# Key tokens first in each group, query tokens last, in a fused vision-tower kernel

## The reference

```python
h = tok(x, channel_weights)                 # patch sums, then 12 -> 192
n = layernorm(h); q, k = n[:, :64], n[:, 64:]
a = softmax(q @ k.T * scale) @ k            # per image
a = transpose(a, (0, 2, 1)).reshape(B, 64, 192) @ proj_w.T + proj_b
h = h + concat([a, k], axis=1)              # keys: only h + layernorm(h)
n = layernorm(h)
s = sigmoid(n @ gate_w.T)                   # best 2 of 4 pairs of experts, then best 2 experts
cw = s of the two chosen, over their sum
out = h + sum_e cw_e * ((silu(n @ w1_e.T) * (n @ w3_e.T)) @ w2_e.T) + the same with the shared expert
```

## Time and profile before

| what | value |
|---|---|
| median of 3 runs | 1877.27 us (1877.26 to 1882.26) |
| the profiled execution | 1882.22 us |
| its span, first to last instruction | 1880.5 us |
| granted clock of TensorE, mean | 0.925 |
| DMA | 436.58 MB, mean 232 GB/s |
| PE / DVE / ACT / POOL busy | 84% / 58% / 49% / 38% |

### The profile page before, as it was taken

The page is one execution under the profiler, slowest core; times in us unless marked ns, Lnnn a source line. Parts: engine busy times, 40 slices in busy tenths (PEclk is TensorE's granted clock), DMA queues, the critical chain, the costliest instruction groups (busy, mean ns, idle before and its releaser), DMA issues.

```text
span 1880.5 us, 30301 instructions
## 1 busy us (share of the span) xinstructions
PE 1584.0 (84%) x9350; PEld 1242.6 (66%) x9350; DVE 1091.8 (58%) x1863; ACT 916.5 (49%) x3047; POOL 705.6 (38%) x687
## 2 busy tenths in 40 slices
...
GB/s 296 314 328 245 299 241 238 278 220 300 254 251 240 255 283 266 255 252 267 234 251 242 255 282 266 254 246 269 286 244 243 257 268 61 47 95 114 86 112 93
DMA packets 120850, 436.58 MB, mean 232 GB/s; under 512 B 20109, under 2 KB 49538, under 8 KB 99182
## 3 DMA queue, kind: packets, MB, share of 16 engines
...
...
HBM read 413.86 MB, written 20.07 MB: 231 GB/s over the span
## 4 chain that ended last, share of the span: by engine, by line
PE 31%; issue 30%; POOL 13%; DVE 11%; DMA 8%; ACT 3%; SPq 3%; ACTq 0%; POOLq 0%; DVEq 0%
PE bank L1427 12%; POOL ffn L655 10%; PE bank L1276 7%; DMA xt<-in_x 7%; PE bank L1447 3%; DVE pooled L842 3%; POOL stat L630 3%; DVE ffn L1190 2%; PE bank L1373 2%; DMA ffn<-cw_rows 2%; SPq L482 1%; PE bank L1385 1%; ACT xt L700 1%; PE bank L1345 1%; PE bank L1405 1%
## 5 line engine op out<-in xcount | busy, mean ns | idle before, releaser
L655 POOL TENSOR_TENSOR ffn<-ffn 128x512 f32<-128x512 f32 (+1 forms) x448 | 515.0, 1152 | 945.9 <-ACT ffn L804 923.2
L1427 PE MATMUL bank<-W2T,ffn 128*128 128x192 f32 (+1 forms) x3600 | 701.5, 334 | 0.0
L1190 DVE TENSOR_TENSOR ffn<-bank,ffn 128x512 f32<-128x512 f32 (+1 forms) x504 | 313.3, 622 | 607.4 <-POOL ffn L655 423.7
L1427 PEld LDWEIGHTS bank<-W2T,ffn 128*128 128x128 f32 (+1 forms) x3600 | 608.7, 192 | 46.3 <-issue 4.8
L842 DVE TENSOR_REDUCE pooled<-xt 128x5 f32<-128x1280 f32 (+2 forms) x296 | 434.4, 1471 | 48.3 <-DMA xt<-in_x 47.2
L804 ACT ACTIVATE ffn<-bank 128x512 f32<-128x512 f32 (+1 forms) x504 | 273.8, 546 | 341.8 <-PE bank L1447 216.4
L700 ACT ACTIVATE xt<-xt 128x256 f32<-128x256 f32 x800 | 323.3, 410 | 184.5 <-DMA xt<-in_x 184.3
L1447 PE MATMUL bank<-tokT,Wx 126*128 126x512 bf16 (+1 forms) x720 | 240.6, 355 | 53.1 <-DVE ffn L1190 52.1
L1447 PEld LDWEIGHTS bank<-tokT,Wx 126*128 126x128 bf16 x720 | 72.1, 101 | 131.7 <-DVE ffn L1190 86.7
L700 ACT ACTIVATION_READ_ACCUMULATOR xt<-xt 128x1 f32 x800 | 155.2, 194 | 0.0
L1276 PE MATMUL bank<-x0h,WT0h 128*128 128x512 f32 x288 | 141.8, 492 | 6.9 <-issue 5.7
...
## 6 DMA issues: line engine op xcount, KB each, us to landing
xt<-in_x SPq DMA_DIRECT2D x168, 1792.0 KB, 7.6
...
out<-stage SPq DMA_DIRECT2D x192, 96.0 KB
...
```

The costliest lines, as they stand in the source:

```text
L655: nc.gpsimd.tensor_tensor(out=cwb[slot][:, 0:n], in0=silu[(g.par + step) % 2][:, 0:n], in1=cwb[slot][:, 0:n], op=ALU.mult).then_inc(scaled, 1)
L1190: v.tensor_tensor(out=h[step % HR][:, 0:n], in0=h_ps(g, step, 1)[:, 0:n], in1=(silu[p] if e == NE else cwb[(c * NE + e) % CW_RING])[:, 0:n ...
L1427: last = mm(o, h[step % HR][:, 128 * t:128 * t + m], W2T[:, e, :], start=(e == 0 and query and t % 2 == 0), stop=(e == NE), skip_group_che ...
```

## The change

- The chunks' order: five key chunks (3, 3, 4, 3 and 3.5 tiles of 128 tokens), then two query chunks. Keys are laid out in runs of 8 tokens per image, so that any number of tiles makes a chunk.
- The plan falls into two. `AK_PLAN` (steps 39 to 60) holds what the key tokens of the **next** group need: tok, V, stats, pow, X, their gates, CK, and half of U. `AQ_PLAN` (steps 0 to 36) holds what the queries of the group **itself** need, attention above all, beside its own key steps. Before group 0's first expert step only `AK_PLAN` runs.
- Tiles: 11 of group g+2 at steps 40 to 61 (`LATE`), 10 of group g+1 at steps 1 to 34 (`EARLY`), the latter in three parts. `SLOTS` is 3.
- Splitting (`Xw`, `Uw`) moves from DVE to POOL; DVE only makes the two replicas.
- Softmax: DVE subtracts each image's maximum (`S`), ACT takes one exponential for eight images (`exp`, twice per group), DVE sums (`sum`).
- `H`: a 72-row stack `Mst` is assembled by DMAs (`stack_mix`, at steps 11 and 17), and one fp32 product replaces three.
- Gates: 28 operations in place of 36, but once for keys (17 tiles) and once for queries (8 tiles). The choice of pairs compares all with all. The coefficient rows are written out by ACT's queue, not SP's.
- The last two second-layer products and the evacuation of a group move into the first steps of the next. `layer2` adds the keys' residual (L1425) in the last step of a chunk, not the first.
- X2T and UTk have one buffer each, not two. The preparation of `CWr` becomes two DMAs.

```diff
-SLOTS = 2
-
-CHUNKS = [(True, 0, 512), (True, 512, 512), (False, 0, 512), (False, 2048, 64)]
-CHUNKS += [(False, 512 * i, 512) for i in (1, 2, 3)]
+
+KT = [3, 3, 4, 3, 3.5]
+CHUNKS = [(False, int(128 * sum(KT[:i])), int(128 * n)) for i, n in enumerate(KT)] + [(True, 0, 512), (True, 512, 512)]
 TT = [(n + 127) // 128 for _, _, n in CHUNKS]
-QCH = 2
-EVAC = [sum((t + 1) // 2 for t in TT[QCH:c + 1]) for c in range(len(TT))]
+QCH = len(KT)
 KPAD = 2176
 NCH = len(CHUNKS)
 STEPS = NCH * EX
+QSTEP = QCH * EX
 GT = 8 + 17
 CWCOL = 1024 + GB * NK
-
-SHARE = {"dve": [(0, 5), (5, 9)], "act": [(9, 12), (12, NP)], "pool": None}
+SLOTS = 3
+
+SHARE_K = {"dve": [(0, 3), (3, 6), (6, 9)], "act": [(9, 11), (11, 13), (13, NP)], "pool": None}
+SHARE_Q = {"dve": [(0, 5), (5, 9)], "act": [(9, 12), (12, NP)], "pool": None}
...
+AQ_PLAN = {
+    0: [("PHT", 0), ("VHw", 0)],
+    1: [("PHT", 1), ("VHT", 0)],
+    2: [("U", 4), ("S", 0)],
+    3: [("U", 5), ("S", 1), ("VHw", 1)],
+    4: [("U", 6), ("S", 2), ("VHT", 1)],
+    5: [("U", 7), ("exp", 0)],
+    6: [("ET", 0), ("sum", 0)],
+    7: [("ET", 1)],
+    8: [("S", 3), ("AH", 0)],
+    9: [("S", 4), ("M", 0)],
+    10: [("S", 5), ("M", 1)],
+    11: [("exp", 1)],
+    12: [("ET", 2), ("sum", 1)],
+    13: [("ET", 3)],
+    14: [("AH", 1)],
+    15: [("M", 2), ("H", 0)],
+    16: [("M", 3), ("H", 1)],
+    17: [("H", 2)],
+    18: [("H", 3)],
+    19: [("stat_q", 0)],
+    20: [("x2", 0), ("H", 4)],
+    21: [("XT", 0), ("H", 5)],
+    22: [("XT", 1), ("H", 6)],
+    23: [("H", 7)],
+    24: [("stat_q", 1)],
+    25: [("x2", 1)],
+    26: [("XT", 2)],
+    27: [("XT", 3)],
+    28: [("GQ", 0), ("GQ", 1)],
+    29: [("G", 0)],
+    36: [("CQ", 0), ("CQ", 1)],
 }
-A_FIRST = 2
-GATES = 36
-for _s in range(12):
-    PLAN[45 + _s] = [("gate", n) for n in range(3 * _s, min(GATES, 3 * _s + 3))] + PLAN.get(45 + _s, [])
-ITEMS = [it for s in sorted(PLAN) for it in PLAN[s]]
-PE_KINDS = ("tok", "V", "PHT", "VHT", "S", "U", "ET", "AH", "M", "X", "H", "XT", "GQ", "G", "C")
-DVE_KINDS = ("tok", "H", "AH", "XT")
+MIX = {11: 0, 17: 1}
+A_FIRST = 39
+AK_PLAN = {
+    39: [("fin", 0), ("tok", 0), ("V", 0)],
+    40: [("stats", 0), ("pow", 0)],
+    41: [("pow", 1)],
+    42: [("stats2", 0), ("pow", 2)],
+    43: [("pow", 3)],
+    45: [("Xw", 0)],
+    46: [("Xw", 1)],
+    47: [("Xw", 2)],
+    48: [("Xw", 3)],
+    49: [("X", 0), ("X", 1)],
+    50: [("X", 2), ("X", 3)],
+    51: [("X", 4), ("X", 5), ("Uw", 0)],
+    52: [("keyG", 0), ("keyG", 1), ("GK", 0), ("Uw", 1)],
+    53: [("Uw", 2)],
+    54: [("Uw", 3)],
+    55: [("U", 0)],
+    56: [("U", 1)],
+    57: [("U", 2)],
+    58: [("U", 3)],
+    59: [("CK", 0), ("CK", 1), ("CK", 2)],
+    60: [("CK", 3), ("CK", 4)],
+}
+GATES = 28
+for _n in range(GATES):
+    AQ_PLAN.setdefault(30 + _n // 5, []).append(("gate_q", _n))
+    AK_PLAN.setdefault(53 + _n // 5, []).append(("gate_k", _n))
+ITEMS = [it for plan in (AK_PLAN, AQ_PLAN) for s in sorted(plan) for it in plan[s]]
+PE_KINDS = ("tok", "V", "PHT", "VHT", "S", "U", "ET", "AH", "M", "X", "H", "XT", "GQ", "G", "GK", "CQ", "CK")
+DVE_KINDS = ("tok", "S", "H", "AH", "XT")
 ROUNDS = [it for it in ITEMS if it[0] in PE_KINDS]
 NR = len(ROUNDS)
 R = {it: i for i, it in enumerate(ROUNDS)}
 BYDVE = [sum(1 for it in ROUNDS[:i + 1] if it[0] in DVE_KINDS) for i in range(NR)]
 BYACT = [i + 1 - BYDVE[i] for i in range(NR)]
 S_IMGS = [(0, 3), (3, 3), (6, 2), (8, 3), (11, 3), (14, 2)]
-LINKS = 57
-
-
-
-
-LATE = {s: i for i, s in enumerate([4, 6, 8, 10, 12, 13, 16, 19, 22, 25, 29, 36, 38, 41, 46, 49, 52, 55, 58])}
-EARLY = {0: 19, 1: 20}
-POOL_TILES = TILES + len(LATE)
+LINKS = 73
+WORKS = 10
+
+
+LATE = {s: i for i, s in enumerate([40, 44, 46, 48, 50, 52, 53, 55, 57, 59, 61])}
+EARLY = {s: len(LATE) + i for i, s in enumerate([1, 5, 8, 12, 16, 20, 23, 27, 31, 34])}
+assert len(LATE) + len(EARLY) == TILES and max(EARLY) + 2 < A_FIRST
...
+def items_at(g, step, left):
+
+    found = [(g, kind, i) for kind, i in AQ_PLAN.get(step, [])] if g.off >= 0 else []
+    if left:
+        found += [(g.plus(1), kind, i) for kind, i in AK_PLAN.get(step, [])]
+    return found
...
+def tile_parts(g, step, left, engine):
+
+    found = []
+    for back in (2, 1, 0):
+        for gt_, t in tiles_at(g, step - back, left):
+            parts = share(gt_, t)[engine]
+            if back < len(parts):
+                found.append((gt_, t, back, parts[back], back == len(parts) - 1))
...
-        CWr = sb("CWr", [128, 3, 4, 128])
+        CWr = sb("CWr", [3 * 2 * CH, 2 * NQ])
...
+            def stack_mix(g, half):
+
+                sp.wait_ge(aux_act, g.at(BYACT[-1], BYACT[R[("M", 2 * half + 1)]]))
+                for m in range(4):
+                    sp.dma_start(Mst[:, 4 * half + m, :],
+                                 Msb[2 * CH * m:2 * CH * (m + 1), half, :]).then_inc(mixed[half], 16)
...
+            def step_dma(g, step, left):
+
+                if step >= 61 and left:
+                    for ahead in ((0, 1) if step == 61 else (2, 3, 4)):
+                        cw_load(g.plus(1), ahead)
+                elif step + CW_AHEAD < STEPS and g.off >= 0:
+                    cw_load(g, step + CW_AHEAD)
+                if step >= LOAD_BEHIND:
+                    landed = tiles_at(g, step - LOAD_BEHIND, left) if g.off >= 0 or step - LOAD_BEHIND >= A_FIRST else []
+                else:
+                    landed = tiles_at(g.minus(1), step - LOAD_BEHIND + STEPS, left + 1)
+                for gt_, t in landed:
+                    load_after(gt_, t)
...
+            def split(g, part, n):
+
+                val_n, res_n = val[:, :, 0:n], res[:, :, 0:n]
+
+                def rounded(out, in_):
+                    one = ones[0:HT, :].unsqueeze(2).to_broadcast([HT, UNITS, n])
+                    return nc.gpsimd.tensor_tensor(out=out, in0=in_, in1=one, op=ALU.mult)
+
+                if part == 1:
+                    work(g, rounded(SPT[:, :, 0, 0, 0:n], val_n))
+                    work(g, nc.gpsimd.tensor_tensor(out=res_n, in0=val_n, in1=SPT[:, :, 0, 0, 0:n], op=ALU.subtract))
+                else:
+                    work(g, rounded(SPT[:, :, 0, 1, 0:n], res_n))
+                    nc.gpsimd.tensor_tensor(out=SPT[:, :, 0, 2, 0:n], in0=res_n, in1=SPT[:, :, 0, 1, 0:n],
+                                            op=ALU.subtract).then_inc(split_done, 1)
+
+            def scaled_tokens(g, row):
...
+                if kind == "exp":
+                    act.wait_ge(aux_dve, g.at(BYDVE[-1], BYDVE[R[("S", 3 * i + 2)]]))
+                    nc.scalar.activation(E[:, :, NQ:TOK], E[:, :, NQ:TOK], ACT.Exp).then_inc(exp_done, 1)
+                    return
...
+                elif kind in ("CK", "CQ"):
+                    n = 64 if (kind, i) == ("CK", 4) else 512
+                    st = cw_stage[(kind, i)][:, 0:n]
+                    nc.scalar.copy(st, ps[0:NE, 0:n]).then_inc(aux_act, 1)
+                    at = 512 * i + (1024 if kind == "CK" else 0)
+                    act.wait_ge(aux_act, g.at(BYACT[-1], BYACT[r]))
+                    act.dma_start(cw_rows[g.par, :, at:at + n], st)\
+                       .then_inc(cw_out[2 if kind == "CQ" else min(i, 1)], 16)
...
-                elif kind == "S_max":
+                elif kind in ("Xw", "Uw") and i == 3:
+                    dve.wait_ge(split_done, g.at(2, 1 if kind == "Xw" else 2))
+                    replicate(g, x_rep if kind == "Xw" else u_rep)
+                elif kind == "S":
                     b0, nb = S_IMGS[i]
-                    r = R[("S", i)]
-                    dve.wait_ge(aux_full, g.at(NR, r + 1))
-                    v.tensor_reduce(out=sums[:, 0, b0:b0 + nb],
-                                    in_=aux[g.bank(r)][0:NQ, 0:nb * NK].rearrange("p (b k) -> p b k", b=nb),
-                                    axis=AX.X, op=ALU.max, negate=True).then_inc(max_ready, 1)
+                    scores = ps[0:NQ, 0:nb * NK].rearrange("p (b k) -> p b k", b=nb)
+                    link(g, v.tensor_reduce(out=sums[:, 0, b0:b0 + nb], in_=scores, axis=AX.X, op=ALU.max, negate=True))
+                    v.tensor_tensor(out=E[:, b0 % 8:b0 % 8 + nb, NQ:TOK], in0=scores,
+                                    in1=sums[:, 0, b0:b0 + nb].unsqueeze(2).to_broadcast([NQ, nb, NK]),
+                                    op=ALU.add).then_inc(aux_dve, 1)
+                elif kind == "sum":
+                    dve.wait_ge(exp_done, g.at(2, i + 1))
+                    link(g, v.tensor_reduce(out=sums[:, 1, 8 * i:8 * i + 8], in_=E[:, :, NQ:TOK], axis=AX.X, op=ALU.add))
...
-                    for q in range(3):
-                        last = mm(ps[:, 0:D], CWr[:, q, i % 4, :], Msb[:, i // 4, D * q:D * q + D],
-                                  start=False, stop=(q == 2))
+                    last = mm(ps[:, 0:D], CWr[:, :], Mst[:, i, :], start=False, stop=True)
...
+            def ffn_pe(g, left, first=False):
                 for step in range(STEPS):
```

(20 more changed lines are left out.)

551 lines of the change are left out of this document (237 added, 314 removed).

## The result

The changed kernel takes 1926.15 us, median of 4 executions (1923.98 to 1933.19), against 1877.26 us of the kernel before in the same session: ratio 1.0261, 95% interval 1.0229 to 1.0292, slower. The forecast was 1843 us with a range of 1782 to 1905: wrong in sign, and outside the range by 21 us. The profiled execution took 1933.19 us for a span of 1931.4.

A forecast was written before the change was run, and what follows sets the result against it. PE was taken as the bound. Span: 200 + 205.5 (group 0) + 5 x 208 + 7.8 (hiccup) + 205 (group 6) + 178 (group 7) + 9.7 (tail) = 1846; + 1.7 - 4.9 = 1843 us, range 1782 to 1905.

The forecast's parts named there:

- The prologue: Before the first multiplication: 132 us until group 0's tiles are summed, then 68 of key stages, 200 instead of 285.3.
- Rival (d): The prologue shrinks less because tile loads set it: 230 us, in all 1873 us; chance 0.05.
- Loads of the engines: Steady group: DVE 134 us, ACT about -3 of 116.8, POOL 10 more than its 77.9.
- PE 182: PE's work in a steady group: 105 us beside keys, 77 beside queries, 182 instead of 188, with 6.2 off for H.
- The powers, "+7": Pows beside key steps 40 to 43: their 17.5 us leave a hole of 10, 7 more than now, per group.
- The stage waits, "-1 for the rest": Other holes of a steady group: smoother placing against tighter engines in key steps, 1 us taken off.
- +10 for exp and other waits: Group 7, which now carries attention: 140.3 + 28 + 10 for these waits = 178 us.
- The stack's transfers, "cost 0": DMAs that stack M for H lie behind work of two or more steps: cost 0; uncovered, some 3 us, twice.
- (a): Groups stay within 205 to 212 us, the prologue's gain less what groups 7 and 6 give back: 1820 to 1868; chance 0.42.
- (c): Key steps, 0 to 44, set by DVE, ACT and POOL in turn: 35 us of holes, group 217, 1897; chance 0.28.
- (b): PE stays full: holes below 20 us because DVE and ACT have room, group 200, 1795; chance 0.20.
- (e): DVE operations standing still for POOL hit the gates: group +5 us, 1873; chance 0.05.

The follow-up runs named there:

- e7: Kernel after, with only five of fourteen columns summed for each of the ten tiles taken in key steps 1 to 36: 1919.4 us.
- e8: Kernel before, with only the projection's second part made one 72-row matmul in place of three of 128, its operand stacked by eight transfers: 1870.1 us.
- e11: Kernel after, with two further idle matmuls in each of a group's eight H, as many as before the change: 1953.7 us.
- e13: e12 with the transposes ET of each half together one step behind the exp and its sum: 1880.0 us, ratio 0.9996.
- e1: Kernel after, with its six GpSimd powers per group made multiplications by 1e-6: 1829.0 us.
- e2: Kernel before, with its GpSimd powers made multiplications by 1e-6: 1842.8 us.
- e9: Kernel after, key plan reordered only: statistics at step 43, powers at 44 to 47, what hangs on them later and closer together: 1873.8 us.
- e12: Kernel after, with e9's key plan and a query plan with XT one step later and GQ, G at 29 to 31: 1853.5 us, ratio 0.986.
- e3: Kernel after, with both kinds of Exp made Copy, so that ScalarE loads no table in the loop: 1929.1 us.
- e5: Kernel before, with four further unused GpSimd powers per group, one in each of key steps 46 to 49: 1915.4 us.

## Why the prediction was wrong, by its own steps

| step of the forecast | forecast | profile after |
|---|---|---|
| first multiplication | 200 | 199.2 |
| group 0 | 205.5 | 220.6 |
| groups 1 to 5 | 1047.8 | 1097.4 |
| PE busy in group 4, beside keys / queries | 105 / 77 | 112.1 / 77.2 |
| PE idle in group 4 | 26 | 29.1 |
| group 6 | 205 | 211.3 |
| group 7 | 178 | 188.8 |
| tail | 9.7 | 14.1 |
| span | 1846 | 1931.4 |

**The prologue** was right in the sum and in both parts (132 and 68; measured 135.0 and 64.2, at a DMA share of 0.93). Rival (d) is out.

**Loads of the engines** were right: DVE 134 forecast, 135.4 measured; POOL 88, 86.5; ACT 114, 110.6. The tile sums, the largest of them, decided nothing in group 4: e7 took 15 us of DVE and 7 of ACT out of it and left its length.

**"PE 182"** failed as a term. PE was busy 189.3 us, and all of the excess lies beside the keys. H's records were really gone (31 fewer), but e8 shows that nothing is won by it in groups 1 to 5 of the old order, and e11 that 3.0 us are won in the new one (mean of groups 1 to 5; 3.5 in group 4) where 6.2 were booked. The idea that failed is that busy time is work at a fixed price: in e8 10 records took 2.40 us at 0.50 where 16 had taken 2.30. In "HAM oscillation — how this bites in real kernels" of "TensorE: Matmul & The Clock Gate" the Trainium skill says that gaps on PE make the clock fall, and that the next batch starts cold. The traces here agree: in e13 PE idles 3.20 us and the records behind it run at 0.50. I had read the granted clock of each window and put no price on it.

**The powers, "+7"**, decided that the new order is slower than the old, but the forecast had them nearly right. It had their place, their queue and GpSimd's 4.1 us a step, a hole of 10 and 7 more than now. Made cheap, they give back 11.3 us per group in the new order and 4.9 in the old (e1, e2, means of groups 1 to 5), 6.4 more; moved to queries they give 8.4, and 52 us in all (e9), where the forecast had 7 for each of seven groups, 49. What was wrong is the form: it was priced as PE's idle time alone, and in group 4 4.2 of the 10.5 us are PE's busy time (189.3 for 185.1 in e1) at a lower granted clock (0.94 for 0.97). The size is off in group 0 alone, where e1 gives 17.6.

**The stage waits, "-1 for the rest"**, is the step that failed most. I set smoother placing against tighter engines and called it even. With the powers made cheap in both orders, a group of the new one should have been 7 us shorter by the forecast (6.2 of H and this 1). It is 3.4 longer (208.2 for 204.8, e1 against e2). With 3.0 for H, the rest is +6.4 us a group where the sum has -1. The table puts it beside the keys, where the attention now stands; that it is the attention's waits is argued from this place, and what sets them is shown only in part. The query plan's order (XT one step later behind its x2, and GQ, G and the gates behind it; e12 against e9 doesn't part them) is worth 20 us in all, 1.9 for each of groups 1 to 5. The exponential's 3.6 us on ScalarE were right in place and measured 4.5 at step 6, but taking them out only moves the wait (e3). Group 7's "+10 for exp and other waits" was short in the same way: 188.8 for 178, 181.8 in e3 and 182.6 in e12.

**The stack's transfers, "cost 0"**, held in the kernel after, but barely: e3 took 2.8 and 2.5 us out of the steps ahead and met a wait of 4.1 us there. The "some 3 us" of an uncovered landing was too little: behind a tile load, at a DMA share of 1.03, the four transfers took 12 us from the first issue to the end of the wait.

**Together**, the span is 85 us over the forecast. Groups 1 to 5 have 49.6 of it, 9.9 each: 7.4 the rest, 3.2 H, and the powers 0.6 the other way. (Each is a difference of means over five groups of single executions, so one as small as 0.6 says nothing.) Group 0 has 15.1, group 7 10.8, group 6 6.3, the tail 4.4. Of the rest's 7.4 us the query plan's order explains 1.9; the other 5.5 stay open, and no run looked into the tail.

**Rivals.** (a), the likeliest, needed groups of 205 to 212 us; they took 215 to 225. (c) had the sign, the place (steps 0 to 44) and nearly the size of a group (217 for 218.4), though its 1897 us is 29 short. Its mechanism, engines setting steps by their loads, is refuted by e7 for the tile sums; for the powers it is the single long instruction in order that counts, 2.90 us against steps of 2 to 3 us (e5, e9). (b) fell with H. (e), DVE standing still for POOL, has no sign in DVE's total; single operations do stand: L1180, 128x32 values, takes 1.02 us in group 4, beside a scaling of POOL, where its neighbours take 0.2.
